# Edge lists laid out on 128 partitions in place of 125

## What is computed

```
h = max(layernorm(x), 0);  x = x + sage(sage(sage(h)))        # three layers: mean over the edges, two products each
h = max(layernorm(x), 0);  x = x + gat(h, src, dst)           # attention: softmax over each node's edges, 4 heads
h = max(layernorm(x), 0);  x = x + rk(h, edge_attr, src, dst) # four steps, each summed over edges src->dst and dst->src
h = max(layernorm(x), 0);  x = x + rel(h, edge_type, norm)    # a product per node and edge type, summed over the edges
```

## Time and profile before

| | us |
|---|---|
| median of 3 runs | 18223.73 |
| lowest and highest | 18201.41, 18237.62 |
| profiled execution: span from first to last instruction | 18199.8 |
| of it: F scatters on POOL, 125.7 to 1440.9 | 1315.2 |
| of it: four stretches of R scatters (50, 40, 140, 620) | 78.3, 62.5, 245.2, 1024.5 |

### The profile page before, as it was taken

The page is one execution under the profiler, slowest core; times in us unless marked ns, Lnnn a source line. Parts: engine busy times, 40 slices in busy tenths (PEclk is TensorE's granted clock), DMA queues, the critical chain, the costliest instruction groups (busy, mean ns, idle before and its releaser), DMA issues.

```text
span 18199.8 us, 134071 instructions
## 1 busy us (share of the span) xinstructions
PE 9887.9 (54%) x41175; PEld 6958.0 (38%) x41175; DVE 6104.5 (34%) x10064; ACT 2627.5 (14%) x4408; POOL 13173.8 (72%) x13148
## 2 busy tenths in 40 slices
PE   6503545555558864455554555545555555549755
PEld 2303434443423353344443444334443344434443
DVE  8601111111168875222222222222222222236422
ACT  0000111111137632011111111111111111110011
POOL 5877777777777788777776777777777777760377
PEclk8655565555589987555555555555555555559755
DMA  1101121121123332111112211122122221217422
GB/s 36 22 3 49 52 51 52 52 52 52 49 64 106 105 82 61 50 53 52 53 53 55 53 53 53 53 56 53 52 53 54 54 53 53 53 55 295 183 53 57
DMA packets 591326, 1154.17 MB, mean 63 GB/s; under 512 B 256151, under 2 KB 323359, under 8 KB 564758
## 3 DMA queue, kind: packets, MB, share of 16 engines
q0 software_dynamic: 420480, 761.05, 17.1%
q1 hardware_dynamic: 166659, 383.98, 5.9%
q10 hardware_dynamic: 3600, 1.51, 0.0%
HBM read 831.58 MB, written 312.20 MB: 63 GB/s over the span
## 4 chain that ended last, share of the span: by engine, by line
POOL 71%; issue 23%; PE 4%; DVE 1%; DMA 1%; ACT 0%; POOLq 0%; SPq 0%; ACTq 0%; DVEq 0%
POOL rows L466 55%; POOL list_r L450 6%; POOL list_f L450 6%; POOL rows L477 4%; PE ps L1250 4%; PE ps L1089 0%; PE ps L1143 0%; DMA rows<-table,rows_F 0%; DVE work L1030 0%; DMA work<-in_edge_attr_4x_dram 0%; DVE work L1024 0%; DMA rows<-table,rows_R 0%; DVE work L1033 0%; PE ps L1160 0%; DMA table<-work 0%
## 5 line engine op out<-in xcount | busy, mean ns | idle before, releaser
L1143 PE MATMUL ps<-rows,onehot 128*128 128x128 f32 (+1 forms) x22880 | 5411.7, 411 | 6220.9 <-DVE rows L811 4163.4
L1143 PEld LDWEIGHTS ps<-rows,onehot 128*128 128x128 f32 x22880 | 4666.5, 301 | 7483.3 <-issue 4832.3
L466 POOL DMA_INDIRECT rows<-table,rows_F x6160 | 5921.1, 961 | 1993.7 <-issue 1873.3
L466 POOL DMA_INDIRECT rows<-table,rows_R x3520 | 3347.7, 951 | 1080.0 <-issue 1071.5
L520 ACT COPY work<-ps 128x1188 f32 x1430 | 1641.8, 1148 | 13682.6 <-PE ps L1149 13675.4
L797 DVE TENSOR_TENSOR onehot<-iota,list_F 128x512 f32<-128x512 f32 x1980 | 1285.4, 690 | 3112.1 <-ACT work L520 3112.1
L1132 PE MATMUL ps<-naught 128*128 128x396 bf16 x4290 | 1601.2, 508 | 1208.4 <-issue 1208.4
L466 POOL DMA_INDIRECT rows<-rel_table,rows_F x880 | 834.8, 949 | 1015.2 <-DMA rel_table<-list_R 747.3
L811 DVE TENSOR_TENSOR rows<-rows,list_F 128x512 f32<-128x512 f32 x880 | 616.4, 700 | 2450.2 <-DMA rows<-table,rows_F 2450.2
L811 DVE TENSOR_TENSOR rows<-rows,list_R 128x512 f32<-128x512 f32 x880 | 615.3, 699 | 2433.7 <-DMA rows<-table,rows_R 2433.7
L450 POOL DMA_INDIRECT list_r<-list_R,rows_R x850 | 1151.2, 1354 | 259.2 <-issue 259.2
(11 more groups left out here) (206 smaller groups left out, 5231.1 us busy)
## 6 DMA issues: line engine op xcount, KB each, us to landing
rel_table<-list_R SPq DMA_DIRECT2D x196, 1024.0 KB, 3.8
rows<-table,rows_F POOLq DMA_INDIRECT x6160, 2.5
gat_rows<-rows SPq DMA_DIRECT2D x220, 264.0 KB, 2.1
rows<-gat_rows SPq DMA_DIRECT2D x220, 264.0 KB
rows<-table,rows_R POOLq DMA_INDIRECT x3520, 2.5
rows<-gat_table,rows_F POOLq DMA_INDIRECT x880, 2.6
rows<-rel_table,rows_F POOLq DMA_INDIRECT x880, 2.5
list_f<-list_F,work POOLq DMA_INDIRECT x850
```

Source lines behind the costliest of these rows:

```text
L466: pool.indirect_dma_start(out=rows[:, t % UNROLL, 0:FEAT], out_offset=None, in_=from_table, in_offset=bass.IndirectOffsetOnAxis(ap=rows_of ...
L1143: ins = mm(into, onehot[:, s, :], rows[:, s, 0:width], start=False, stop=True, skip_group_check=True)
```

## The change

The edges lie on 128 partitions in 831 columns. That is 118 places more than there are edges; all 118 are at the end of the last partition, behind LIVE = 713 columns. They are given node numbers past the last one, so they count in no block, and their records go to 118 spare rows behind each list in DRAM, which nobody reads. The turn of the loops has 6 chunks; 84 chunks make EW = 840 columns of work. An input is loaded with three DMAs (112, 15 and 1 partitions). Five memsets write the unused places beforehand, and the loads wait for them (`raw_blank`). POOL waits for `spare_ready` before it sends column 713 of F, and before R. The last pause has SI − 23 = 61 times 10 scatters, cut off at 831.

```diff
-EP = 125
-EC = EDGES // EP
+EP = P
+EC = -(-EDGES // EP)
 CT = 10
-CHUNKS = EC // CT
-CU = 5
+CU = 6
+CHUNKS = -(-EC // (CT * CU)) * CU
 CI = CHUNKS // CU
 CB = CT * BLOCKS
+EW = CHUNKS * CT
 SU = 10
-SI = EC // SU
+SI = -(-EC // SU)
+SPARE = EP * EC - EDGES
+LIVE = EC - SPARE
+PART_RUNS = [(0, 112), (112, P - 1)]
...
-PAUSES = {"sage0 F": 5, "sage1 F": 4, "sage2 F": 14, "peak F": 62}
+PAUSES = {"sage0 F": 5, "sage1 F": 4, "sage2 F": 14, "peak F": SI - 23}
...
-        list_dram = {"F": dram("list_f", (P * TILES, W)), "R": dram("list_r", (P * TILES, W))}
+        list_dram = {"F": dram("list_f", (P * TILES + SPARE, W)), "R": dram("list_r", (P * TILES + SPARE, W))}
...
+            sp.wait_ge(raw_blank, 5)
+            for view, arr, n in ((src_i, src, 1), (dst_i, dst, 1), (type_i, edge_type, 1),
+                                 (norm_f, edge_weight.rearrange("e o -> (e o)"), 1),
+                                 (attr_f, edge_attr.rearrange("e h o -> (e h o)"), HEADS)):
+                for lo, hi in PART_RUNS:
+                    sp.dma_start(view[lo:hi, 0:EC * n], arr[lo * EC * n:hi * EC * n].rearrange("(p c) -> p c", p=hi - lo)).then_inc(raw_loaded, 16)
+                sp.dma_start(view[P - 1:P, 0:LIVE * n], arr[(P - 1) * EC * n:EDGES * n].rearrange("(p c) -> p c", p=1)).then_inc(raw_loaded, 16)
...
-                    sp.wait_ge(scattered[q], 16 * SI * (k + 1))
+                    sp.wait_ge(scattered[q], 16 * len(range(q, EC, SU)) * (k + 1))
...
+            nc.gpsimd.iota(spare_i, pattern=[[1, SPARE]], base=LIVE, channel_multiplier=EC).then_inc(iotas, 1)
...
+                if c == LIVE:
+                    pool.wait_ge(spare_ready, 1)
                 scatter("F", c)
...
+                    pool.wait_ge(spare_ready, 2)
-                    for c in range(done * SU, (done + PAUSES[name]) * SU):
+                    for c in range(done * SU, min(EC, (done + PAUSES[name]) * SU)):
                         scatter("R", c)
...
+            for view, n, at in ((src_i, 1, ROWS), (dst_i, 1, ROWS), (type_i, 1, 0), (norm_f, 1, 0.0), (attr_f, HEADS, 0.0)):
+                v.memset(view[:, LIVE * n:], at).then_inc(raw_blank, 1)
...
+            st(v.tensor_scalar(spare_i, spare_i, float(EDGES - 1), 0.0, ALU.subtract, ALU.max))
+            st(v.tensor_scalar(tile_spare, spare_i, 1.0, float(P * TILES - 1), ALU.min, ALU.mult))
+            st(v.tensor_tensor(spare_i, spare_i, tile_spare, ALU.add), False)
-            dve.wait_ge(raw_loaded, 80)
+            dve.wait_ge(raw_loaded, 16 * 15)
...
                 dve.wait_ge(records_ready, CI * (k + 1))
+                spare = to_row[key][:, LIVE:EC]
+                v.tensor_tensor(spare, spare, spare_i, ALU.add).then_inc(spare_ready, 1)
```

More of the change, by code:

```diff
@@ L60 @@
 SLOPE = 0.2
-assert EP * EC == EDGES and CI * CU * CT == EC and SI * SU == EC and GB * GI == BLOCKS
+assert 0 <= SPARE < EC and CI * CU * CT == EW and EC <= EW and GB * GI == BLOCKS
 assert TILES % 8 == 0 and TILES // 8 <= P and CB <= 512
@@ L201, in place @@
             return v if dt == F32 else v.bitcast(dt)
[L203 to L212, removed]
+        src_i, dst_i, type_i = (place(at, EW, I32) for at in (0, EW * 15 + 450, EW * 16 + 450))
+        norm_f = place(EW * 3, EW)
+        attr_f = place(EW * 4, EW * HEADS)
+        hi_f = {"F": place(EW * 8, EW), "R": place(EW * 9, EW)}
+        key_t = place(EW * 10, EW, I32)
+        pos_f = place(EW * 11, CU * CT)
+        self_f = place(EW * 12, EW)
+        spare_i = place(EW * 13, SPARE, I32)
+        tile_spare = place(EW * 13 + 610, SPARE)
+        pos_all = place(EW * 14, EW)
+        earlier, ones, zeros = (work[:, at:at + n // 2].bitcast(BF16) for at, n in ((EW * 15, P), (EW * 15 + 64, P), (EW * 15 + 128, 512)))
         key_n = place(3200, CU * CT, I32)
         key_q = place(3200 + CU * CT, CU * CT, I32)
[L215 to L219, removed]
+        to_row = {"F": place(0, EW, I32), "R": rows_of_list["R"][0:EP, 0:EW]}
+        member_bf = work[0:EP, 850:850 + CU * CB // 2].bitcast(BF16).rearrange("p (s n) -> p s n", s=CU)
+        rank_t = work[0:EP, 2330:2330 + CB]
+        carry = work[:, 2830:2830 + BLOCKS]
+        small = work[:, 2880:2880 + 5 * BLOCKS].rearrange("p (k b) -> p k b", k=5)
         small_i = work[:, 3150:3150 + BLOCKS].bitcast(I32)
@@ L231, in gnn_kernel @@
         half_of = [ps[:, SLOT_BANKS * n:SLOT_BANKS * (n + 1), :] for n in range(2)]
+        raw_blank = sem("raw_blank")
+        spare_ready = sem("spare_ready")
         raw_loaded = sem("raw_loaded")
@@ L356, in _ @@
         def _(sp):
[L357 to L360, removed]
+            sp.wait_ge(raw_blank, 5)
[5 more added lines that the diff above has]
+                sp.dma_start(view[P - 1:P, 0:LIVE * n], arr[(P - 1) * EC * n:EDGES * n].rearrange("(p c) -> p c", p=1)).then_inc(raw_loaded, 16)
             sp.wait_ge(pads_ready, 2)
             for key in "FR":
-                sp.dma_start(list_dram[key].rearrange("(p t) w -> p (t w)", p=P),
+                sp.dma_start(list_dram[key][0:P * TILES, :].rearrange("(p t) w -> p (t w)", p=P),
                              lists[key][:, :, :].rearrange("p t w -> p (t w)")).then_inc(pads_written, 16)
@@ L378, in load_list @@
                 for q in range(SU):
-                    sp.wait_ge(scattered[q], 16 * SI * (k + 1))
+                    sp.wait_ge(scattered[q], 16 * len(range(q, EC, SU)) * (k + 1))
                 sp.dma_start(lists[key][:, :, :].rearrange("p t w -> p (t w)"),
-                             list_dram[key].rearrange("(p t) w -> p (t w)", p=P)).then_inc(list_loaded, 16)
+                             list_dram[key][0:P * TILES, :].rearrange("(p t) w -> p (t w)", p=P)).then_inc(list_loaded, 16)
             n = 0
@@ L625, in _ @@
             dve.sem_inc(fetch_read, 1)
-            dve.wait_ge(iotas, 4)
+            for view, n, at in ((src_i, 1, ROWS), (dst_i, 1, ROWS), (type_i, 1, 0), (norm_f, 1, 0.0), (attr_f, HEADS, 0.0)):
+                v.memset(view[:, LIVE * n:], at).then_inc(raw_blank, 1)
+            dve.wait_ge(iotas, 5)
             st(v.tensor_copy(iota[:, :], iota_i[:, :]), False)
@@ L657, in records @@
                 for key, near, far in (("F", dst_i, src_i), ("R", src_i, dst_i)):
-                    rec = lists[key][0:EP, 0:EC, :]
+                    rec = lists[key][0:EP, 0:EW, :]
                     if key == "R":
@@ L666, in records @@
                     st(v.tensor_copy(rec[:, :, 3:3 + HEADS], attr_f.rearrange("p (c h) -> p c h", h=HEADS)))
-                rec = lists["F"][0:EP, 0:EC, :]
+                rec = lists["F"][0:EP, 0:EW, :]
                 st(v.scalar_tensor_tensor(out=rec[:, :, 1], in0=src_i, scalar=float(RELS), in1=type_i, op0=ALU.mult, op1=ALU.add))
```

## The result

The changed kernel takes **17782.68 us** in the median of 4 runs (17753.97 to 17787.33), the kernel before beside it 18222.82 (18201.41 to 18237.62). The ratio is 0.9754, with a 95% interval of 0.9742 to 0.9766. The forecast was 17766, the range 17715 to 17880. The profiled span is 17752.1 us, 447.7 less than before.

A forecast was written before the change was run, and what follows sets the result against it. Bound: indirect DMAs on POOL, number times cost each, except where POOL stops for a table. Gains 3 + 231.5 + 12.1 + 0 + 34.0 + 177.5 = 458 us from span 18199.8 gave 17742; plus 23.9, 17766 us (range 17715 to 17880).

The forecast's parts named there:

- What a scatter costs: Each scatter of 128 records on POOL was taken at a gather's 944 ns instead of 1187, 0.243 us less.
- Start, −3: Before the first scatter: faster input loads gain about 5.7 us, chunk changes shift it, together 3 us less.
- F, −231.5: Stretch of F scatters: 850 at 1.547 us become 831 at 0.243 less each, 1315.2 to 1083.7 us.
- contention left as it is per scatter: Assumption for all scatters: time lost to DVE's operations stays the same per scatter; 47 us in the F stretch before.
- sage0 −12.1: Pause after sage0, 50 R scatters: 78.3 us becomes 66.2, the table write just covered.
- sage1 0: Pause after sage1, 40 R scatters: 62.5 becomes 52.8, but POOL waits some 11 us for the table; nothing gained.
- sage2 −34.0: Pause after sage2, 140 R scatters: 245.2 us becomes 211.2, the PEAK table being there earlier.
- Peak pause, −177.5: Pause after the peak gathers: 620 scatters in 1024.5 us become 601 in 847.0, 4 us behind rk0's table.
- the table of rk0 is issued: In the peak pause: rk0's table write issues at 7175.73, takes 15.6, so is there 842.7 us after the pause began.
- Only 19 scatters fewer: Rival: scatters stay at 1187 ns, only the 38 saved in both directions and the start count; 64 us, 18160; chance 10%.
- Late table: Rival: denser scatters stretch the attention stage, delivering rk0's table late; at most all peak gain lost, 17944; chance 5%.
- Slower: Rival: a scatter's price rises with the engines carrying records, 0.259 us above 1187 ns; 18589 us; chance 3%.

The follow-up runs named there:

- the new counts: The changed kernel with its R scatters shared out over the four pauses as 47, 47, 102, 635 instead of 50, 40, 140, 601: 17734.47 us, ratio 0.9741.

## Why the prediction was right, point by point

- **What a scatter costs.** Right in kind and nearly in size: 958 ns for the 944 taken from the gathers. The 14 ns are 12 us over F.
- **Start, −3.** It is −5.2. DVE goes on at 25.11, as forecast, and there is no wait for the attributes.
- **F, −231.5.** It is −202.4; this is the term that was mis-sized, by 29 us. Of these, 12 are the 14 ns. The other 17 are the step "contention left as it is per scatter": it was (1056.4 − 850 x 1.187) = 47 us over 850 scatters and is 859.6 − 831 x 0.958 = 63.5 over 831. With 125 records in the new layout it is 1035.99 − 831 x 1.187 = 50, so it came with the 128-record scatters and not with the layout. DVE's work has its own length, which would explain that faster scatters do not meet less of it; why they lose more to it is not shown. I had allowed for the opposite, 35 us less.
- **sage0 −12.1, sage1 0, sage2 −34.0.** They are −11.1, −0.4 and −30.8. The wait that was named for sage1, 11 us, is 9.73.
- **Peak pause, −177.5.** It is −195.5, and the reasons were partly wrong. I expected the scatters to end 4 us behind the table and said that a wait of over 20 us would speak against the forecast; it is 43.83. The scatters took 785.3 us for 847: the same step failed the other way, contention there was 835.3 − 620 x 1.187 = 99 us and is 602.1 − 601 x 0.958 = 26. Of these 73 us, 22 are four scatters fewer held by the norm's long operations, as POOL is done before them. The rest came with the 128-record scatters: with 125 records the new layout still has 810.11 − 601 x 1.187 = 97. But the table ends this pause now, and with the table where I had left it, 842.7, the cheaper scatters would have given only the 4 us from 847.0. The other 14 are a second step that failed, "the table of rk0 is issued" 827.1 after the pause began: it was issued after 815.0, and landed 2 us faster. As the table of the stage's lengths above shows, the 125-record scatters had stretched that stage, and the 128-record ones hardly do.
- **The sum** was 458 and is 445: two errors of 29 and 18 us with opposite signs and different causes. That part of the accuracy is luck. Of the 17 us by which the forecast misses the median, 10 are in the span; the rest is that the median now lies 30.6 above the profiled span, where I had added the 23.9 of before.
- **The rivals.** *Only 19 scatters fewer* was priced at 64 us; the new layout with 125 records is worth 55, and has the 1187 ns. *Late table* did not come on normal chips. *Slower* did, on the slow chip, for two variants of the changed kernel, but through another mechanism than the one I gave: the scatters themselves stayed cheap, and PE stood beside them. My 3% had looked for it in the wrong place.

## What to carry to other kernels

Give an indirect DMA a partition count that 16 divides. Look in the packets for how many engines carry the data; a prime count such as 127 puts everything on one. A few padded places are cheap against it: here 118 spare records with rows of their own. When the longest engine's work gets shorter, look at once which of its pauses was cover for somebody else, and share out anew what is left: here the new counts brought another 32 us. And measure on more than one chip: on the slow chip a variant of this change was 5% slower than the kernel before.

## What the runs showed of the hardware that was not expected

- POOL's time for an indirect DMA depends on the longest list of one engine, 837 ns at 1 record, 958 at 8, 1178 at 25, 2538 at 127, and hardly on the number of records: 127 take 2.6 times as long as 128.
- Only some of DVE's long operations (128x6272 f32, 6.69 us) hold a scatter. With the new counts, six scatters of the peak pause last 6.39 to 6.75 us, one beside each of the six operations with two inputs; the copy at 6810.06 and the reductions at 6831.10 and 6851.49 hold none.
- Scatters from 5 engines' lists (125 records) made the attention stage 13 to 16 us longer, those from 16 engines' (128 records) 1 to 7.
- One chip ran the kernel before in 20118 us and not 18200. Its 880 gathers of an rk0 stage took about 1247 us in place of 1105 with the same duration of a gather. Most of the difference is in waits of 3.0 us that the profile calls "remote". On it PE stood for up to 50 us at a time beside the 128-record scatters of the attention stage, and did not beside the 125-record ones of the kernel before; the cause is open.
